# A decoder layer with latent attention, cross attention and routed experts: head values transposed by VectorE instead of TensorE, and latents computed as two column tiles with a shortened decision chain

## What is computed

```python
q = x @ Wq; k = x @ Wk; v = x @ Wv
latent_kv = (k + v) @ W_down_kv                      # 64 latents
k_rec = latent_kv @ W_up_k; v_rec = latent_kv @ W_up_v
scores = einsum('bhqd,bhkd->bhqk', qh, kh) * scale   # 16 heads of 16
scores = clip(scores) * exp(-0.01 * 0.01 * abs(i - j))
attn = softmax(scores); out = einsum('bhqk,bhkd->bhqd', attn, vh)
x = x + out @ Wo                                     # x layer-normed before
```

## Time and profile before

| | us |
|---|---|
| device time, median of 3 runs | 612.98 (612.12 to 613.30) |
| device time of the profiled execution | 613.19 |
| its span | 611.40 |
| first scores of the head stage (L709) | 58.88 |
| TensorE busy | 554.1 (91%) |
| ScalarE busy | 399.1 (65%) |
| VectorE busy | 374.5 (61%) |
| GpSimd busy | 212.6 (35%) |
| from 100 to 200 us: TensorE, ScalarE, VectorE, GpSimd busy | 100.0, 95.2, 58.4, 51.2 |

### The profile page before, as it was taken

The page is one execution under the profiler, slowest core; times in us unless marked ns, Lnnn a source line. Parts: engine busy times, 40 slices in busy tenths (PEclk is TensorE's granted clock), DMA queues, the critical chain, the costliest instruction groups (busy, mean ns, idle before and its releaser), DMA issues.

```text
span 611.4 us, 14232 instructions
## 1 busy us (share of the span) xinstructions
PE 554.1 (91%) x4551; PEld 300.2 (49%) x4552; DVE 374.5 (61%) x1002; ACT 399.1 (65%) x568; POOL 212.6 (35%) x238
## 2 busy tenths in 40 slices
PE   3995999999999999999999899999999769899960
PEld 2442333333333333333336677767655556666640
DVE  5796555565555655555554488787888624444564
ACT  4477999999999999999993555645443723232310
POOL 4000693494049500000003242280275714444450
PEclk9997899999999999999999999999989979999995
DMA  9923333444444444433404730000022234443746
GB/s 258 367 91 67 71 73 71 75 77 77 78 77 78 76 73 74 74 73 71 84 27 131 200 86 3 2 1 2 2 86 87 90 105 129 119 135 123 254 165 206
DMA packets 53595, 60.20 MB, mean 98 GB/s; under 512 B 10769, under 2 KB 44690, under 8 KB 53554
## 3 DMA queue, kind: packets, MB, share of 16 engines
q1 hardware_dynamic: 46546, 46.19, 31.8%
q0 software_dynamic: 3792, 10.36, 4.7%
q10 hardware_dynamic: 3216, 3.15, 1.5%
HBM read 22.17 MB, written 18.61 MB: 67 GB/s over the span
## 4 chain that ended last, share of the span: by engine, by line
PE 75%; DMA 8%; DVE 7%; issue 4%; ACT 4%; POOL 1%; DVEq 0%; ACTq 0%; POOLq 0%; SPq 0%
PE ps L719 21%; PE ps L709 20%; PE ps L1105 8%; DMA x_slots<-val,place_i 6%; PE ps L1122 4%; PE ps L761 2%; PE ps L862 2%; PE ps L930 2%; PE ps L1097 2%; PE ps L728 2%; DVE ftmp L1776 2%; PE ps L637 1%; DMA qT<-y_tok 1%; PE ps L880 1%; PE ps L898 1%
## 5 line engine op out<-in xcount | busy, mean ns | idle before, releaser
L1632 DVE TENSOR_TENSOR ps<-ps,kstack 128x128 f32<-128x128 f32 (+3 forms) x256 | 123.9, 495 | 103.6 <-PE ps L709 103.5
L1253 ACT ACTIVATE pT<-ps 128x1024 f32<-128x1024 f32 x128 | 124.9, 1022 | 6.3 <-PE ps L709 2.6
L709 PE MATMUL ps<-qstack,kstack 96*128 96x512 bf16 x352 | 93.1, 388 | 4.6 <-issue 4.6
L719 PE MATMUL ps<-pT,vcur 128*32 128x256 f32 x1024 | 80.5, 387 | 0.0
L1253 ACT ACTIVATE xn<-ps 128x1024 f32<-128x1024 f32 x64 | 65.6, 1024 | 9.3 <-PE ps L709 8.2
L590 POOL DMA_INDIRECT y_tok<-ftmp,dest_i x47 | 45.1, 959 | 60.2 <-DVE ftmp L2054 59.9
L1253 ACT ACTIVATE xnT<-ps 128x1024 f32<-128x1024 f32 x64 | 65.2, 1019 | 0.2
L1105 PE MATMUL ps<-parts,xnT 128*128 x188 | 53.9, 411 | 6.4 <-issue 3.7
L709 PEld LDWEIGHTS ps<-qstack,kstack 96*128 96x128 bf16 x352 | 29.2, 98 | 54.7 <-issue 15.6
L1430 ACT ACTIVATE oT<-ps 128x128 f32<-128x128 f32 x47 | 13.0, 278 | 63.1 <-PE ps L1105 63.1
L563 POOL TENSOR_TENSOR resid<-resid,projb 128x512 f32<-128x512 f32 x8 | 10.1, 1266 | 122.4 <-DVE xn L1969 121.8
(11 more groups left out here) (299 smaller groups left out, 965.1 us busy)
## 6 DMA issues: line engine op xcount, KB each, us to landing
qstack<-parts SPq DMA_DIRECT2D x132, 64.0 KB, 2.3
x_slots<-wcur SPq DMA_DIRECT2D x1, 6016.0 KB, 21.0
kT<-x_slots SPq DMA_DIRECT2D x47, 128.0 KB, 2.2
kstack<-parts SPq DMA_DIRECT2D x132, 32.0 KB, 2.0
early<-parts SPq DMA_DIRECT2D x60, 64.0 KB, 2.3
resid<-in_x_dram SPq DMA_DIRECT2D x4, 512.0 KB, 5.3
parts<-in_L_ffn_Wg_dram SPq DMA_DIRECT2D x16, 128.0 KB, 2.3
parts<-in_L_ffn_Wu_dram SPq DMA_DIRECT2D x16, 128.0 KB, 2.3
```

The costliest lines, as they stand in the source:

```text
L709: nc.tensor.matmul(ps[:, score_bank(g3, kt) + g, :], kstack[g3][:, kt * P:(kt + 1) * P], qstack[g3][:, 1 - first, 512 * g:512 * (g + 1)], ...
L719: mm = nc.tensor.matmul(ps[2 * HD * g:2 * HD * (g + 1), 6 + r, 0:256], vcur[:, r, kt, :], pT_ring[kt % 4][:, 256 * g:256 * (g + 1)], start ...
L1253: nc.scalar.activation(pT_ring[kt % 4], two_banks(score_bank(g3, kt)).rearrange("p a n -> p (a n)"), ACT.Exp, bias=-SHIFT).then_inc(s_exp, 1)
L1632: nc.vector.tensor_tensor(blk, blk, within[:, side, 4 * P - n:] if side == 0 else within[:, side, 0:n], ALU.mult)\
```

## The change

In the head loop the 256 columns of a column tile are taken as eight runs of 32 queries, so that tile g of a group holds queries 32 g to 32 g + 31 of each of the eight query tiles. VectorE then transposes the result in blocks of 32 x 32 on its way out of PSUM, which gives rows of queries as `att` needs them; TensorE's transposes, `out_transposes`, and the semaphores `s_ot` and `s_on` go. In the front the latents are computed as two column tiles of 64, each over one half of the chunk's columns; `wkvd_sb` holds the weights once, `latT` has 256 columns, and keys and values take the halves of the tokens from the two halves of the partitions. In the decision, the memset in front of GpSimd, two small instructions and one drain go, two memsets are added, and the reductions are reordered.

```diff
-        wkvd_sb = early[:, 2 * KD * D:2 * KD * D + KD * P].rearrange("p (k n) -> p k n", k=KD)
+        wkvd_sb = early[:, 2 * KD * D:2 * KD * D + KD * LAT].rearrange("p (k n) -> p k n", k=KD)
-        latT = sb("latT", [P, CHUNK])
+        latT = sb("latT", [P, HCHUNK])
...
+        caps = sb("caps", [P, 2])
...
                 for k in range(KD):
-                    mm = nc.tensor.matmul(ps[:, 0, :], wkvd_sb[:, k, :], xnT[:, k, :], start=(k == 0), stop=(k == KD - 1))
+                    for n in range(2):
+                        mm = nc.tensor.matmul(ps[n * LAT:(n + 1) * LAT, 0, 0:HCHUNK], wkvd_sb[:, k, :],
+                                              xnT[:, k, n * HCHUNK:(n + 1) * HCHUNK], start=(k == 0), stop=(k == KD - 1),
+                                              tile_position=(0, n * LAT))
...
-                for n in range(KD):
-                    rows = slice(n * LAT, (n + 1) * LAT)
-                    mm = nc.tensor.matmul(ps[:, 4 + n, :], wup_sb[rows, 0, n * P:(n + 1) * P], latT[rows, :],
-                                          start=True, stop=True, tile_position=(n * LAT, 0))
+                for m in range(KD):
+                    for n in range(2):
+                        rows = slice(n * LAT, (n + 1) * LAT)
+                        mm = nc.tensor.matmul(ps[:, 4 + n, m * HCHUNK:(m + 1) * HCHUNK], wup_sb[rows, 0, m * P:(m + 1) * P],
+                                              latT[rows, :], start=True, stop=True, tile_position=(n * LAT, 0))
...
-                    after(pe, s_on, n - 1)
+                    after(pe, s_ob, n - 1)
                 for g in range(4):
-                    mm = nc.tensor.matmul(ps[2 * HD * g:2 * HD * (g + 1), 6 + r, 0:256], vcur[:, r, kt, :],
-                                          pT_ring[kt % 4][:, 256 * g:256 * (g + 1)], start=(kt == 0), stop=(kt == ST - 1),
-                                          tile_position=(0, 2 * HD * g))
+                    out_g = ps[2 * HD * g:2 * HD * (g + 1), 6 + r, 0:256].rearrange("p (t q) -> p t q", q=2 * HD)
+                    mm = nc.tensor.matmul(out_g, vcur[:, r, kt, :],
+                                          pT_ring[kt % 4].rearrange("p (t g q) -> p g t q", g=4, q=2 * HD)[:, g, :, :],
+                                          start=(kt == 0), stop=(kt == ST - 1), tile_position=(0, 2 * HD * g))
                 mm.then_inc(s_pv, 1)
-
-            def out_transposes(n, r):
-
-                pe.wait_ge(s_ob, n + 1)
-                for c in range(2):
-                    mm = nc.tensor.transpose(ps[:, 6 + r, 256 + c * P:256 + (c + 1) * P], obT[:, c * P:(c + 1) * P], ident[:])
-                mm.then_inc(s_ot, 1)
...
-                    if kt == 4 and not first:
-                        out_transposes(n - 1, 1 - r)
...
                 out_begin()
-                out_transposes(n, 1)
                 out_first()
...
-            nc.scalar.copy(wkvd_sb.rearrange("p k (a n) -> p k a n", n=LAT),
-                           ps[:, 5, 0:KD * LAT].rearrange("p (k n) -> p k n", k=KD).unsqueeze(2)
-                           .to_broadcast([P, KD, P // LAT, LAT])).then_inc(s_wd, 1)
+            nc.scalar.copy(wkvd_sb, ps[:, 5, 0:KD * LAT].rearrange("p (k n) -> p k n", k=KD)).then_inc(s_wd, 1)
...
-                nc.scalar.copy(latT[:], ps[:, 0, :]).then_inc(s_lat, 1)
+                nc.scalar.copy(latT[:], ps[:, 0, 0:HCHUNK]).then_inc(s_lat, 1)
...
             nc.vector.memset(red[:], 0.0)
+            nc.vector.memset(caps[:, 0:1], (SPAN + SHIFT) ** 2 / 1.02)
+            nc.vector.memset(caps[:, 1:2], (SPAN_LOW - SHIFT) ** 2 / 1.02 * S * S)
...
             norm_max(NCHUNK - 1)
-            nc.vector.drain()
+            dve.wait_ge(s_kmean, 2)
+            nc.vector.tensor_reduce(red[0:2 * HD, 3:4], ps[0:2 * HD, 4, 0:B * KD], AX_X, ALU.max)
+            dve.wait_ge(s_nred, NCHUNK)
             nc.vector.tensor_reduce(red[0:P // 2, 0:1], nmaxs[0:P // 2, :], AX_X, ALU.max)
             nc.vector.tensor_reduce(red[P // 2:P, 1:2], nmaxs[P // 2:P, :], AX_X, ALU.max)
-            dve.wait_ge(s_kmean, 2)
-            nc.vector.tensor_reduce(red[0:2 * HD, 3:4], ps[0:2 * HD, 4, 0:B * KD], AX_X, ALU.max)
...
-            nc.vector.tensor_reduce(red[:, 5:6], sqok[:].rearrange("p t c -> p (t c)"), AX_X, ALU.max)
-            nc.vector.drain()
-            nc.vector.memset(fl[:, 8:9], 0.0).then_inc(s_red, 1)
+            nc.vector.tensor_reduce(red[:, 5:6], sqok[:].rearrange("p t c -> p (t c)"), AX_X, ALU.max).then_inc(s_red, 1)
             dve.wait_ge(s_reda, 1)
-            nc.vector.tensor_tensor(fl[:, 0:1], reda[:, 0:1], reda[:, 1:2], ALU.mult)
-            nc.vector.tensor_tensor(fl[:, 1:2], reda[:, 0:1], reda[:, 3:4], ALU.mult)
+            nc.vector.tensor_tensor(fl[:, 0:2], reda[:, 0:1].to_broadcast([P, 2]), reda[:, 1:4:2], ALU.mult)
...
-            nc.vector.tensor_scalar(fl[:, 5:6], fl[:, 0:1], (SPAN + SHIFT) ** 2 / 1.02, None, ALU.is_le)
-            nc.vector.tensor_scalar(fl[:, 6:7], fl[:, 1:2], (SPAN_LOW - SHIFT) ** 2 / 1.02 * S * S, None, ALU.is_le)
+            nc.vector.tensor_tensor(fl[:, 5:7], fl[:, 0:2], caps[:], ALU.is_le)
...
             def read_out(n, r):
                 dve.wait_ge(s_pv, ST * (n + 1))
-                after(dve, s_ot, n)
-                nc.vector.tensor_copy(obT[:], ps[:, 6 + r, 0:256]).then_inc(s_ob, 1)
-
-            def normalise(n, r):
-
-                dve.wait_ge(s_ot, n + 1)
-                o = ps[:, 6 + r, 256:512].rearrange("p (c g d) -> p g c d", c=2, g=4)
-                nc.vector.reciprocal(rinv8[:].rearrange("p (g c) -> p g c", c=2), o[:, :, :, HD])
+                nc.vector.transpose(obT[:], ps[:, 6 + r, 0:256]).then_inc(s_ob, 1)
+
+            def normalise(n):
+
+                dve.wait_ge(s_ob, n + 1)
+                o = obT[:].rearrange("p (t d) -> p t d", d=2 * HD)
+                nc.vector.reciprocal(rinv8[:], o[:, :, HD])
                 nc.vector.drain()
-                nc.vector.tensor_tensor(att[:, ds(n // H * ST, ST), ds(n % H * HD, HD)].rearrange("p (g c) d -> p g c d", c=2),
-                                        o[:, :, :, 0:HD],
-                                        rinv8[:].rearrange("p (g c) -> p g c", c=2).unsqueeze(3).to_broadcast([P, 4, 2, HD]),
-                                        ALU.mult).then_inc(s_on, 1)
+                nc.vector.tensor_tensor(att[:, ds(n // H * ST, ST), ds(n % H * HD, HD)], o[:, :, 0:HD],
+                                        rinv8[:].unsqueeze(2).to_broadcast([P, ST, HD]), ALU.mult)
```

More of the change, by code:

```diff
@@ L33 @@
 CHUNK = CT * P
+HCHUNK = CHUNK // 2
 NCHUNK = T // CHUNK
@@ L297, in decoder_layer @@
         s_fs = sem("s_fs"); s_diag = sem("s_diag"); s_exp = sem("s_exp"); s_pv = sem("s_pv"); s_vcur = sem("s_vcur")
-        s_ob = sem("s_ob"); s_ot = sem("s_ot"); s_on = sem("s_on"); s_att = sem("s_att")
+        s_ob = sem("s_ob"); s_att = sem("s_att")
         s_cT_ps = sem("s_cT_ps"); s_cT = sem("s_cT"); s_ck_ps = sem("s_ck_ps"); s_ck = sem("s_ck")
@@ L654, in values_up @@
                 for i in range(CT // 2):
-                    for n in range(KD):
-                        rows, t = slice(n * LAT, (n + 1) * LAT), n * (CT // 2) + i
-                        mm = nc.tensor.matmul(ps[:, 6 + n, i * D:(i + 1) * D], latT[rows, t * P:(t + 1) * P],
+                    for n in range(2):
+                        rows = slice(n * LAT, (n + 1) * LAT)
+                        mm = nc.tensor.matmul(ps[:, 6 + n, i * D:(i + 1) * D], latT[rows, i * P:(i + 1) * P],
                                               wup_sb[rows, 1, :], start=True, stop=True, tile_position=(n * LAT, 0))
@@ L1201, in queries, with by_channel, squared @@
                 nc.scalar.mul(qT[:, :, c * CHUNK:(c + 1) * CHUNK], two_banks(2), ATTN_SCALE).then_inc(s_q, 1)
-            def squared(t, c, first, semaphore, scale=1.0):
-                nc.scalar.activation(squares[:, t, :, c * CHUNK:(c + 1) * CHUNK], two_banks(first), ACT.Square, scale=scale,
-                                     accum_out=sqsum[:, t, c:c + 1]).then_inc(semaphore, 1)
+            def by_channel(halves):
+                return halves.rearrange("p n (k q) -> p k n q", k=KD)
+            def squared(t, c, src, semaphore, scale=1.0):
+                dst = squares[:, t, :, c * CHUNK:(c + 1) * CHUNK]
+                if t == 1:
+                    dst = dst.rearrange("p k (n q) -> p k n q", n=2)
+                nc.scalar.activation(dst, src, ACT.Square, scale=scale, accum_out=sqsum[:, t, c:c + 1]).then_inc(semaphore, 1)
             def keys_up(c):
```

11 lines of the change are left out of this document (6 added, 5 removed).

## The result

The changed kernel takes 607.53 us in the median of 4 runs (603.02 to 607.95), the kernel before 613.14 on the same chip (4 runs, 612.12 to 615.48). The ratio on record is 0.9865, with an interval of [0.9825, 0.9905]: 8.3 us less, between 5.8 and 10.7. The two medians by themselves are only 5.6 us apart; with four executions each, spread over 4.9 and 3.4 us, the size is not known better than that. Set against the 612.98 of the prediction the ratio gives 604.7; the median itself lies 0.7 us above the range given. The profiled execution took 607.95 us, with a span of 606.20 (before: 613.19 and 611.40). It is the slowest of the four, and shows a gain of 5.2 only.

A forecast was written before the change was run, and what follows sets the result against it. TensorE was taken to bound the head stage, so time taken off it counts in full. The terms -8.2 + 0.1 - 1.6 - 0.3 = -10.0 us gave 603.0 us against the median 612.98, range 600.8 to 606.8.

The forecast's parts named there:

- hidden anyway: Head loop: the transposes' time is hidden already, so only the front gains; 611.1 us, chance 0.04.
- Part 1: Head loop: without TensorE's transposes a head takes 7.88 us instead of 8.15; -8.2 us over 31 heads.
- the sentence on SyncE: Head loop: SyncE issues a head's twelve stack loads in 7.59 us, under 7.88; costed at nothing.
- the cover of 0.29 a head: Head loop: what SyncE's stack loads still gain on TensorE per head, 0.29 us where it was 0.56.
- VectorE's transpose: Head loop: replaces the 0.41 us copy, taken as 0.45 us, far end 0.70; no cost to the period.
- rival 3: Weighted-value matmuls in the head loop: the broken-up moving operand slows them; 628 us at 20%, chance 0.06.
- rival 1: Head loop: ScalarE's exps or VectorE's longer step hold the period at about 8.0 us; 606.6 us, chance 0.14.
- Part 2: Front: latents as two column tiles save 0.8 us a chunk on TensorE, effective in chunks 0 and 2; -1.6 us.
- the amount that the prediction set beside its sum: Latents: an added tiling-mode change drains TensorE, making the saving 0.1 us a chunk smaller, 0.2 in all.
- Part 3: Decision: GpSimd starts 0.16 us sooner and two small instructions behind it go, -0.14; -0.3 us in sum.
- rival 2: Front: latents give nothing at the end, 604.6 us; clock variants 604 (same rise moment) or 600.2 (never fell); chance 0.08.
- Nothing behind the head stage changes, and it moves along.: Stages after the head loop: they keep their length and only start sooner; no term in the sum.

The follow-up runs named there:

- e10: The changed kernel with both edits: six extra TensorE matmuls around the decision wait, and head 1's query rows loaded by GpSimd; 603.64 us, ratio 0.9855.
- e2: The kernel before with only the two-tile latents and the shorter decision; 611.33 us, ratio 0.9954.
- e3: The changed kernel once more, nothing edited; 604.94 us, ratio 0.9857 against the kernel before.
- e1: The kernel before with only VectorE's transposes, the broken-up operand and no TensorE transposes in the loop; 610.24 us, ratio 0.9936.
- e4: The changed kernel with the six query transfers of head 1's stack issued by GpSimd instead of SyncE; 605.23 us, ratio 0.9848.
- e5: The changed kernel with thirteen stack transfers a head instead of twelve; 621.11 us, one run.
- e7: The changed kernel with two TensorE transposes of other data put back behind the loop; 604.16 us, one run.
- e11: The changed kernel again, nothing edited; 607.39 us, ratio 0.9895 against the kernel before.
- e6: The kernel before with thirteen stack transfers a head instead of twelve; 624.88 us, one run.
- e9: The changed kernel with six extra TensorE matmuls on other data around the decision wait; 605.96 us, ratio 0.9864.
- e12: Repeat of e10 beside the unedited changed kernel on the same chip; 605.05 us, ratio 0.9833.

## Why the prediction was right, and where it was off

**The direction and the size.** 603.0 was forecast, with 600.8 to 606.8; the first measurement has 607.53 with the kernel before at 613.14, the two later ones 604.94 against 614.0 and 607.39 against 614.54. The gains are 8.3, 8.8 and 6.4 (by the ratios), the forecast 10.0. The way and the mechanism came out as forecast; the size is 12 to 36% short of it. Neither a rival on the other side nor "hidden anyway" came true: both parts gain by themselves.

**Part 1, -8.2.** The period was right. Neighbouring read-outs late in the loop are 308.42 - 300.54 = 7.88 us apart, and over the 30 intervals of the kernel with both edits they are (306.00 - 69.3) / 30 = 7.89; before it is (317.23 - 72.8) / 30 = 8.15. So the transposes cost what was said, 0.26 a head. The measured loop of the first profile gains 6.7, not 8.1, and this comes out as: 30 intervals with 0.26 are -7.9; the time behind the last read-out of the loop -0.1; waits for stacks +1.8, predicted as nothing; the lower clock at the loop's start, 4.2 us of it for 5.6, half of the difference, -0.7. The sum is -6.9.

- *The step that failed* is the sentence on SyncE: 7.59 under 7.88, "costed at nothing". The 7.59 was read at 136.5 us, behind the last of the long transfers, and holds from there on; as the bound it was named rightly, as thirteen transfers show. Early in the loop it is not the number. In the changed kernel 53 transfers, from one long one to another, take 110.14 - 73.67 = 36.47 us, or 8.26 for twelve, which is over 7.88: SyncE loses its lead there and TensorE waits 1.8 us. The long ones are in the kernel before too (1.55 is its longest); there 69 transfers take 115.33 - 68.84 = 46.49 us, or 8.09 for twelve, just under 8.15, and TensorE never waits. So the cover of 0.29 a head was gone in the first third of the loop, and the term that was put at nothing measured +1.8 us. A margin has to be set against the queue's rate in the slowest stretch of the loop, not against a regular one, and against how much lead there is at the start.
- VectorE's transpose: 0.44 for 0.45 taken, between the ends of 0.41 and 0.70. The Trainium skill (VectorE: DVE Perf Modes, The three transpose paths) has 311 ns for 128x128 bf16; this is twice the columns, in float32 out of PSUM, and no run here has the page's form.
- The broken-up moving operand, rival 3 at 0.06: L726 takes 0.379 a matmul and 1.00 for sixteen, as before. Zero was right.
- ScalarE as the limit, rival 1: its waits for VectorE's product come to some 2 us in the whole loop (a row of the table of waits each of 1.5 and 0.6), and in e10, where no stack is late, the period is 7.89. Rival 1 named a period of 8.0 by ScalarE or VectorE; that it came out near it, (308.42 - 70.0) / 30 = 7.95, has another cause: it holds the 1.8 us of waits for stacks.

**Part 2, -1.6.** It measured -1.6, in the chunks that were named: -0.9 up to chunk 2's transposes, to which chunk 1 added nothing, then -1.60 at chunk 2's values and -1.60 at chunk 3's (50.83 for 52.43). One chunk of latents took 1.01 us for 1.0. But at full clock the gain of a chunk is 0.7 and not 0.8, since the query matmuls behind the latents take 3.70 us for 3.60; they do so in e2, e3 and e10 too, while e1, with the old latents, has 3.60. By the Trainium skill (TensorEngine Tiling (Array Packing), Key Properties) a change of tiling mode drains TensorE. The trace agrees, with 0.1 us a chunk, the amount that the prediction set beside its sum and left out of it. The total is right by luck of 0.1 us: chunk 0's latents started 0.10 us sooner (15.23 for 15.33), chunk 0 gave 0.8 and chunk 2 0.7.

**Part 3, -0.3.** It gave 0.6. GpSimd starts 54.03 - 50.83 = 3.20 us behind the start of chunk 3's values, 3.67 before; from GpSimd's end to the flag's conversion it is 0.92, where 1.05 stood. The second difference is the 0.14 predicted. The first was taken as 0.16 and is 0.47: the new order of the reductions, "saves a drain, the two new memsets cost as much", came with 0.3 us more. No run takes the new order, the drain and the memsets apart. The memsets stand in VectorE's row at 0.01 to 0.02 us from each other and cost next to nothing.

**The clock, rival 2.** "If it rises at the same moment although the loop begins 1.9 us sooner, half of that is lost": no profile has it at quite the same moment. Six profiles have the change's TensorE program up to the loop (the first, e3, e4, e5, e7, e11). The clock rises at 60.8 to 63.3 us in them, where it rose at 64.5 and 65.3 in the two of before. In three of the six it stayed low for 6.8 to 7.0 us of the loop, in the other three for 4.2 to 4.5, against 5.6 and 5.7 before. So over these the clock neither gave nor took much, and the term of nothing was right in the mean and off by up to 0.7 us either way. The other half of that rival, 600.2 if it never fell, is what e10 made: from the first scores to the first read-out it takes 12.2 us, against 14.0 in the kernel before.

**"Nothing behind the head stage changes, and it moves along."** In the first pair of profiles this fell: no instruction changed but the two transposes, and yet 289.5 us became 293.3. It doesn't hold up as a loss of the change. Over the profiles of the two kernels the stretch is 289.5 and 291.7 before, and 293.3, 290.4, 291.6 and 292.4 after (e4 has the same program there). Taking in every profile whose program behind the loop is that of before (e2, e6) or of the change (e1, e5, e9, e10, e12), the means are 291.4 of four and 291.7 of nine, while single ones lie between 288.4 and 295.7. So the step was right in the mean, and what was missing is a scatter of some microseconds in the range.

**The sum as measured**, in means of the two profiles of before and the four of after: loop -6.7, front -3.0, behind it +1.3, together -8.4, for -8.1, -1.9 and 0. The last two are not firm: the front's -3.0 is -2.5 over the eleven profiles with the one front or the other that lack the added matmuls.

**What stays open.** Why four or five transfers take 0.9 to 2.0 us to issue, and why only early in the loop. Why the signal of the last counting matmul comes 3.5 to 6.4 us late in nine profiles of fourteen. And why the clock falls 10 to 11 us behind the loop's end in six profiles (the change three times, e1, e4, e5) and 9.0 behind it in e6, and not in seven others (before, e2, e7 to e10, e12); the missing transposes alone don't explain it, and no run here settled what does.

## What to carry to other kernels

When TensorE is the bound and work is taken off it, compare the new period with every other engine's per-iteration time, the queues that issue transfers included; where the margin is a few per cent, ask how much lead the queue has at the start, and read its rate in several stretches of the loop, the early ones above all. Two causes that cover for each other (a slow clock at the start and a late queue) must be removed together before either shows. And a saving of one per cent in an early stage moves everything behind it against the stretches of low clock, and the part behind the loop scattered over 7 us here whatever the kernel: leave some microseconds in the range for that, and judge by stages in the profile rather than by the total.

## What was not expected of the hardware

- A transfer inside the chip takes SyncE 0.59 us to issue, and 0.04 stand between two. Early in the loop, from 67 to 124 us, every 15th to 23rd takes 0.9 to 2.0 us, for 32 KB as for 64 KB; later ones don't.
- TensorE's eight full-array query matmuls took 3.70 us behind two column tiles of 64, and 3.60 behind full-array matmuls.
- VectorE started 0.04 us after the record of the matmul that it waits for had ended in five profiles, and 3.5 to 6.4 us after it in nine, with the clock full in seven of them.
- A wait of 2.45 us on TensorE was followed by 3.4 us at the lower clock, in which the work of 2.97 us took 79.36 - 74.85 = 4.51, so that the wait cost another 1.5.
- The places of the low stretches differ from one execution to the next: three executions of the change have them at 54.0, 52.4 and 53.0 us, at 323.7, 322.1 and 322.7, and then at 450.0 and 487.5, 441.5 and 482.5, 442.2 and 459.2.
- A matmul whose moving operand is eight runs of 32 float32, 512 bytes apart, with four column tiles reading interleaved runs, is as fast as with one run of 256: 379 ns in both kernels.
